# Merged weights written in place, two weight parts and a widening moved, in a GNN kernel

## What is computed

```
edge_index = stack([src, dst])
# layer 0
xw   = x @ W.T
deg  = segment_sum(1, col);  dinv = rsqrt(deg)
h    = segment_sum(dinv[row] * dinv[col] * xw[row], col) + b
x    = layernorm(x + gelu(batch_norm(h)) + x)
# layer 1, twice: basis1, att1 ... then basis2, att2 ...
w    = einsum('rb,bio->rio', att, basis)      # 2 relations from 30 matrices of 512 x 512
msg  = sigmoid(x[col] @ gate_w[r]) * x[col] @ w[r],  r by edge type
out  = segment_sum(msg, row) + x @ root + bias
```

## Time and profile before

| | before |
|---|---|
| median of three runs | 308.99 us (306.59 to 311.51) |
| the profiled execution, its own time | 306.44 us |
| its span, first to last instruction | 304.6 us |
| PE busy | 272.2 us (89%) |
| PE's weight loads busy | 180.6 us (59%) |
| DVE busy | 158.6 us (52%) |
| ACT busy | 87.9 us (29%) |
| POOL busy | 50.9 us (17%) |
| DMA, moved | 73.64 MB, mean 242 GB/s |
| mean granted clock of TensorE | 0.982 |

### The profile page before, as it was taken

The page is one execution under the profiler, slowest core; times in us unless marked ns, Lnnn a source line. Parts: engine busy times, 40 slices in busy tenths (PEclk is TensorE's granted clock), DMA queues, the critical chain, the costliest instruction groups (busy, mean ns, idle before and its releaser), DMA issues.

```text
span 304.6 us, 4601 instructions
## 1 busy us (share of the span) xinstructions
PE 272.2 (89%) x1687; PEld 180.6 (59%) x1687; DVE 158.6 (52%) x338; ACT 87.9 (29%) x143; POOL 50.9 (17%) x92
## 2 busy tenths in 40 slices
PE   0789997988999976679999999999998999999991
PEld 0673442443667632355766664677786777777770
DVE  6788889886647839835301413342342235334443
ACT  3351031002548694462440142114103252000000
POOL 5431013000590037100000000000008200011111
PEclk9999999999799998999999999999999999999997
DMA  6999999999499999959949797766003300001112
GB/s 155 219 413 373 381 421 413 396 396 386 174 310 332 421 420 421 352 224 347 377 183 390 281 418 292 290 267 270 2 0 87 88 1 0 0 2 34 34 34 67
DMA packets 12803, 73.64 MB, mean 242 GB/s; under 512 B 2000, under 2 KB 2243, under 8 KB 4588
## 3 DMA queue, kind: packets, MB, share of 16 engines
q1 hardware_dynamic: 11330, 70.82, 61.1%
q0 software_dynamic: 1104, 2.36, 3.0%
q10 hardware_dynamic: 346, 0.17, 0.3%
HBM read 72.05 MB, written 1.28 MB: 241 GB/s over the span
## 4 chain that ended last, share of the span: by engine, by line
PE 69%; DMA 11%; DVE 9%; issue 5%; DVEq 1%; ACT 1%; POOL 1%; SPq 0%; POOLq 0%; ACTq 0%
PE psW L552 15%; PE psM L533 9%; PE psM L534 9%; PE psM L535 9%; DMA basis_ring<-in_L_gnn_basis_dram 8%; PE psM L800 8%; PE psM L820 6%; PE psM L684 3%; DMA xs<-in_x_dram 3%; PE psM L607 2%; DVE B L1118 2%; PE psE L641 2%; PE psM L593 1%; PE psM L763 1%; DVE x_sum L1259 1%
## 5 line engine op out<-in xcount | busy, mean ns | idle before, releaser
L552 PE MATMUL psW<-basis_ring,S 128*32 128x512 f32 x512 | 65.1, 622 | 6.5 <-DMA basis_ring<-in_L_gnn_basis_dram 4.1
L1306 DVE SCALAR_TENSOR_TENSOR zg<-psM,gate,zg 125x512 fp32r<-125x512 f32 x20 | 15.0, 750 | 56.9 <-ACT zg L988 56.9
L552 PEld LDWEIGHTS psW<-basis_ring,S 128*32 128x32 f32 x512 | 13.2, 112 | 35.9 <-issue 21.9
L533 PE MATMUL psM<-w,hlT 128*125 128x512 f32 x80 | 32.4, 405 | 0.1
L534 PE MATMUL psM<-w,hlT 128*125 128x512 f32 x80 | 31.7, 396 | 0.0
L535 PE MATMUL psM<-w,hlT 128*125 128x512 f32 x80 | 31.7, 396 | 0.0
L988 ACT ACTIVATE zg<-psM,gate 125x512 fp32r<-125x512 f32 x20 | 13.8, 689 | 46.3 <-PE psM L535 45.9
L517 POOL DMA_DIRECT2D root_raw<-in_L_gnn_root_dram x16 | 7.9, 502 | 105.7 <-DVE hlT L1336 105.7
L641 PEld LDWEIGHTS psE<-oh_key,oh_src 128*125 128x125 f16 x162 | 14.0, 142 | 19.1 <-issue 12.7
L800 PEld LDWEIGHTS psM<-BB,zg 125*128 125x128 f32 x160 | 23.1, 188 | 3.4 <-issue 2.5
L800 PE MATMUL psM<-BB,zg 125*128 125x320 f32 (+1 forms) x160 | 24.1, 309 | 0.0
(11 more groups left out here) (154 smaller groups left out, 387.9 us busy)
## 6 DMA issues: line engine op xcount, KB each, us to landing
basis_ring<-in_L_gnn_basis_dram SPq DMA_DIRECT2D x64, 1024.0 KB, 7.3
root_raw<-in_L_gnn_root_dram POOLq DMA_DIRECT2D x32, 64.0 KB, 4.3
xs<-in_x_dram SPq DMA_DIRECT2D x1, 1120.0 KB
out_dram<-xs SPq DMA_DIRECT2D x5, 224.0 KB
w_raw<-in_L_gnn_W_dram SPq DMA_DIRECT2D x4, 256.0 KB, 9.7
bias_b<-in_L_gnn_bias_dram POOLq DMA_DIRECT2D x1, 250.0 KB, 3.8
xs<-in_x_dram SPq DMA_DIRECT2D x1, 130.0 KB
out_dram<-xs SPq DMA_DIRECT2D x5, 26.0 KB
```

Of the source, the lines that this page charges most:

```text
L533: nc.tensor.matmul(o, l_hi, r_hi, start=start, stop=False)
L552: m = nc.tensor.matmul(psW[32 * j:32 * j + 32, cc % 2, :], S[:, cc % 2, cc // CH, q].rearrange("p k r -> p (k r)"), ring[:, n % RING, j, : ...
L1306: link(v.scalar_tensor_tensor(out=zg[:, 1, c, r, :], in0=bank(("Z", L, c, r))[0:PC, :], scalar=gate[:, L, c, r:r + 1], in1=zg[:, 0, c, r, ...
```

## The change

- **In place.** `both` is gone. The merges write the full-width weights where the lower part will stand (`w03_full`, `w45_full` share memory with `w03`, `w45`), and already in the column order that blocks 0 to 3 need: the two merge instructions read `half` and `psW` with the step, and `w_high` and `w_low` read and write without one. The merge no longer waits for the upper and lower part of the block before; in its place DVE has the waits for the memory of blocks 4, 5 and from 6 on (`w_free`).
- **Lower part of block 0** goes from POOL (during the loop) to DVE, behind the sums of f = 0.
- **Parts on PE.** Parts 18 and 19 go from the loop (group 25) to behind the degrees, where 20 and 21 stood; 20 and 21 go behind f = 0, and 22 and 23 join 24 and 25 behind f = 1. Parts 10 and 11 move from group 15 to 14. Some steps of L607 and the transposes of the inputs are spread a little differently.
- **Counts widened first.** ACT widens chunks 1 to 3 ahead of copying the last chunk of x @ W.T out of PSUM, and DVE copies the degrees after the first instruction of merge 1, ahead of its other two.
- **Windows.** The registers of the four last windows are read in groups 1 and 13 in place of 0 and 1, and DVE waits for `base_i` one group later.
- **Way back.** The transposes of `hf` for chunks 0 to 3 go quarter by quarter: 16 transposes, of which the 13th is the first to complete a chunk. Chunk 4 follows.

In the diff, cut to its core:

```diff
-        both = sb("w_both", [P, 2, D], F32)
...
-        FIRST_IN = 23
+        FIRST_IN = 21
...
+        def w_full(pp, r):
+
+            b = pp % WBLK
+            return (w03_full[:, b] if b < 4 else w45_full[:, b - 4])[:, r, 1, :]
+
+        def w_free(eng, pp):
+
+            if pp == WBLK - 2:
+                eng.wait_ge(adj_used, T)
+            elif pp == WBLK - 1:
+                eng.wait_ge(root_ready, KC)
+            elif pp >= WBLK:
+                eng.wait_ge(main_full, uses[("Z", 0, NC - 1, R - 1)] + 1)
+
-        TURN_AT = {0: (AHEAD_OF_ATT + 1,), 1: (NC - 1,), 2: (NC, NC + 1), 3: (NC + 2, NC + 3)}
-        XW_AT = (0, 0, 0, 0, 0, 1, 1, 2, 2, 3, 5, 5, 6, 8, 9, 9, 10, 11, 11, 13, 13, 14, 14, 15, 17, 17, 17)
-        PARTS_AT = (0, 0, 0, 0, 2, 2, 4, 4, 6, 6, 6, 8, 8, 10, 10, 12, 12, 14, 14, 14, 16, 16, 18, 18, 18, 20, 20)
+        TURN_AT = {0: (AHEAD_OF_ATT,), 1: (AHEAD_OF_ATT + 1, NC - 1), 2: (NC, NC + 1), 3: (NC + 2, NC + 3)}
+        XW_AT = (0, 0, 0, 0, 0, 1, 1, 2, 2, 3, 5, 5, 6, 8, 9, 9, 11, 11, 12, 13, 13, 14, 14, 15, 17, 18, 18)
+        PARTS_AT = (0, 0, 0, 0, 2, 2, 4, 4, 6, 6, 6, 8, 8, 10, 12, 12, 12, 14, 14, 14, 16, 16, 18, 18, 18, 18, 18)
...
-            for r in range(R):
-                pool.wait_ge(w_hi, r + 1)
-                upper = w_block(0, 0)[:, r, 0, :].bitcast(F32)
-                nc.gpsimd.tensor_tensor(in_q(w_block(0, 0)[:, r, 1, :]), natural(both[:, r, :]), in_q(upper), ALU.subtract) \
-                    .then_inc(w_lo, 1)
...
-            basis_upto(21)
+            basis_upto(19)
...
-                basis_upto((None, FIRST_IN + 2, 27, 27)[f])
+                basis_upto((None, FIRST_IN + 4, 27, 27)[f])
             basis_upto(31)
-            for c in range(NC):
-                pe.wait_ge(gelu_done, KC)
-                wait_free(pe, ("g", c))
-                for f in range(KC):
...
+            for f in range(KC):
+                for c in range(NC - 1):
+                    way_back(f, c)
+            for f in range(KC):
+                way_back(f, NC - 1)
...
-            xw_out(4)
             for c in SUMMED:
                 act.wait_ge(at_sum, SUMMED.index(c) + 1)
                 nc.scalar.activation(AT[:, c], at_sums(c), ACT.Copy).then_inc(at_from_sum, 1)
+            xw_out(4)
...
-                dve.wait_ge(w_hi, R * pp)
-                dve.wait_ge(w_lo, R * pp)
-                v.scalar_tensor_tensor(out=both[:, 0, :], in0=psW[:, 1, :], scalar=mask_h[:, 1:2], in1=half[:, 0, :],
+                w_free(dve, pp)
+                to, first, second = w_full(pp, 0), half[:, 0, :], psW[:, 1, :]
+                if pp < KC:
+                    to, first, second = in_q(to), natural(first), natural(second)
+                v.scalar_tensor_tensor(out=to, in0=second, scalar=mask_h[:, 1:2], in1=first,
                                        op0=ALU.mult, op1=ALU.add).then_inc(w_both, 1)
...
-            w_merge(1)
+            w_merge_first(1)
             wait_full(dve, "deg")
...
+            w_merge_rest(1)
...
-                if f == 1:
-                    w_low(1)
+                if f < 2:
+                    w_low(f)
```

More of the change, by code:

```diff
@@ L717, in _, with way_back @@
                     counts_turned(2 * f + h)
-                basis_upto((None, FIRST_IN + 2, 27, 27)[f])
+                basis_upto((None, FIRST_IN + 4, 27, 27)[f])
             basis_upto(31)
-            for c in range(NC):
-                pe.wait_ge(gelu_done, KC)
-                wait_free(pe, ("g", c))
-                for f in range(KC):
-                    last[0] = nc.tensor.transpose(bank(("g", c))[0:PC, f * P:(f + 1) * P],
-                                                  hf[:, f, c * PC:(c + 1) * PC], ident[:])
-                done()
+            def way_back(f, c):
+                pe.wait_ge(gelu_done, f + 1)
+                if f == 0:
+                    wait_free(pe, ("g", c))
+                last[0] = nc.tensor.transpose(bank(("g", c))[0:PC, f * P:(f + 1) * P],
+                                              hf[:, f, c * PC:(c + 1) * PC], ident[:])
+                if f == KC - 1:
+                    done()
+            for f in range(KC):
[3 more added lines that the diff above has]
+                way_back(f, NC - 1)
             basis_upto(33)
@@ L1091, in w_merge_rest @@
                                             in1=half[:, 1, :], op0=ALU.mult, op1=ALU.add))
-                link(v.stream_shuffle(both[:, 1, :], half[:, 1, :], SWAPPED))
+                to, swapped = w_full(pp, 1), half[:, 1, :]
+                if pp < KC:
+                    to, swapped = in_q(to), natural(swapped)
+                link(v.stream_shuffle(to, swapped, SWAPPED))
                 dve.sem_inc(w_both, 1)
@@ L1099, in w_low @@
                     dve.wait_ge(w_hi, R * pp + r + 1)
-                    block_w = w_block(pp // KC, pp % KC)
-                    lo, full, hi = block_w[:, r, 1, :], both[:, r, :], block_w[:, r, 0, :].bitcast(F32)
-                    if pp < KC:
-                        lo, full, hi = in_q(lo), natural(full), in_q(hi)
-                    v.tensor_tensor(lo, full, hi, ALU.subtract).then_inc(w_lo, 1)
+                    upper, lower = (w_block(pp // KC, pp % KC)[:, r, i, :] for i in range(2))
+                    v.tensor_tensor(lower, w_full(pp, r), upper.bitcast(F32), ALU.subtract).then_inc(w_lo, 1)
             def window_at(w):
@@ L1134, in _ @@
                 one_hots(src.rearrange("p t (k i) -> p t k i", i=2), place_pairs, g * G, G, PLACES)
[L1136 to L1137 removed]
+                first, second = (2 * (g - 2), 2 * (g - 2) + 1) if g >= 2 else (NW - 4, NW - 3)
+                at = [window_at(first)] if g else []
                 one_hots(oh_key[:, g * G % OH:g * G % OH + G].rearrange("p t (k i) -> p t k i", i=2), key_pairs, g * G, G, KEYS) \
                     .then_inc(key_ready, 1)
[L1140 removed]
+                if g:
+                    at.append(window_at(second))
                 if g < 2:
```

29 lines of the change are left out of this document (10 added, 19 removed).

## The result

| | before | changed |
|---|---|---|
| median, first measurement, 4 runs each | 307.79 us (306.21 to 311.51) | 312.42 us (309.51 to 313.19) |
| ratio, 95% interval | | 1.0122 [1.0063, 1.018] |
| median, measured again (experiment e5), 23 and 12 runs | 310.08 us | 310.75 us |
| ratio, 95% interval | | 1.0033 [1.000, 1.0066] |
| profiled execution, own time / span | 306.44 / 304.6 us | 313.19 / 311.3 us; in e5 309.60 / 307.8 us |

A forecast was written before the change was run, and what follows sets the result against it. The stream of basis loads was taken as the bound up to 111 us. Load gap +1.7, root1 -0.9, way back +1.2, merges -0.7 and +0.6 gave +1.9 on the profiled 306.44: 308.3 us, range 303.5 to 312.5.

The forecast's parts named there:

- The gap: Pause in the basis loads near 77 us: grows from 3.8 to 5.5 or 6.5 us; +1.7 us taken, at full clock.
- rival 2: Low clock behind the degrees slows the aggregation, part 20 used after about 86 us, loads pause again: 311.3 us, chance 0.15.
- In the loop: Loop over the edges: DVE gains some 1.3 us, costed at nothing because part 17 lands at 64.37 regardless.
- From part 17 to part 18: PE up to the degrees' end: 25 matmuls take 2.86 us and end at 76.0 where it was 78.8.
- Root1: Its small loads between 83 and 98 us meet fewer basis parts: at best half of 3.6 us goes, -0.9 us taken.
- The way back: Transposes ahead of DVE's first `x_sum`: 13 needed instead of four, +1.2 us, which stay.
- Merges: Steps in DVE's merges: subtractions without the step win -0.7 us, merge instructions with it cost +0.6 us.
- Signs and range: Profile signs such as a load gap over 5 us and part 31 landing at 110.5 to 113; own range 306.8 to 310.5.
- Rival 1: PE's order, not the loads, ends last: PE stops waiting for parts 30 and 31, faster at 304.2 us, chance 0.25.

The follow-up runs named there:

- e5: The changed kernel run again unedited, on a second chip: 310.75 us, ratio 1.0033 to before.
- e2: The kernel before with only the places of parts 18 to 25 moved as in the change: 315.12 us, ratio 1.0129 to before.
- e11: The kernel before with merge 1's sums ahead of the degrees' copy and PE released ahead of the shuffle in every merge: 309.04 us, ratio 0.9959.
- e6: The changed kernel with root1's loads issued later, behind the scale of quarter f = 1: 317.61 us, ratio 1.0128 to before.
- e7: The changed kernel with parts 18 to 21 behind the degrees, 22 and 23 behind f = 0, 24 and 25 behind f = 1: 311.33 us, ratio 1.0083.
- e9: The changed kernel with parts at their places of before and the way back chunk by chunk, without earlier release of PE: 306.04 us, ratio 0.9872.
- e12: The kernel of e8 unedited, run again in another set: 303.92 us, ratio 0.9803 to before.
- e1: The changed kernel with only the parts put back at their places of before: 307.19 us, ratio 0.9899 to before.
- e10: The kernel of e8 with the change's new order of the way back: 304.80 us, ratio 0.9827 to before.
- e8: The changed kernel with parts and way back as before, and PE released ahead of the shuffle in every merge: 303.42 us, ratio 0.9773 to before.
- e3: The changed kernel with the way back chunk by chunk as before: 309.50 us, ratio 0.9992 to before.

## Why the prediction went wrong where it did

The direction was right, the size was not. Two steps of the prediction failed. The gap in the loads was priced with parts 18 and 19 at full clock, +1.7 us; they ran at half clock, and the pause grew by 2.9 us in one profile and by 4.4 us in the other. And four parts together behind f = 1 on a ring of four places were costed at nothing; PE waited 3.2 and 3.9 us for parts 24 and 25, and worked at half clock behind the wait.

The spans differ by 6.7 us in the first profile and by 3.2 us in e5's. Split at the landing of part 31 and at `x_sum`, in us against before:

| | forecast | changed | e5 |
|---|---|---|---|
| part 17 lands | 0 | -1.25 | -0.8 |
| first pause | +1.7 | +4.4 | +2.9 |
| second pause | (rival 2) | +1.8 | +1.3 |
| rest of the stream, root1 | -0.9 | -0.2 | -0.6 |
| part 31 lands | +0.8 | +4.75 | +2.8 |
| from there to `x_sum` | +1.2 | +1.0 | +1.0 |
| behind `x_sum` | -0.1 | +1.0 | -0.6 |
| sum | +1.9 | +6.7 | +3.2 |

The rows down to part 31 are an account of the stream of loads. The second pause is read off the DMA share from 106 to 110 us. "Rest" is what remains.

Read on PE, where the chain runs, the same +4.75 us is another sum. PE asks for part 24 at 94.57 us and not at 94.03, +0.5. It waits 3.9 us for parts 24 and 25. It no longer waits for parts 30 and 31 (0.8 and 1.4 us before), -2.3. What remains, +2.6 us, is work done at half clock behind the wait: part 25 takes 1.93 us and not 1.06, the next ten aggregation matmuls 3.04 and not 1.74. In e5 the four terms are -0.8, +3.2, -2.3 and +2.7, together +2.8.

**In the loop.** "Part 17 lands at 64.37 whatever DVE does" was wrong. It landed at 63.12 (63.58 in e5), PE did not wait for it in the first profile and only 0.40 us in e5. DVE's slow `oh_key` is gone, as forecast: the longest of the 27 takes 0.87 us, not 1.97. The loads come sooner step by step and not at one place: against before, part 5 lands 0.35 us sooner, part 9 0.73 and part 17 1.24. In all profiles with the changed kernel's loop part 17 lands between 62.2 and 63.6 us, in the three with the loop of before (before, e2, e11) between 64.0 and 64.6. Which edit of the loop does it was not tested.

**From part 17 to part 18.** Here the degrees' price failed in one profile of two. I took 2.86 us for the 25 matmuls and 76.0 as their end: they ended at 77.1 in the first profile and at 75.9 in e5. I had kept their duration of before, when the clock fell at 79 us, behind them. The clock fell earlier now, and in the first profile already within the degrees. The Trainium skill (TensorE: Matmul & The Clock Gate, Part 1) says that the place where the clock changes differs from run to run, and has measured it on the change to full clock. The prediction said that no run showed it; the two profiles of one kernel now show it of the fall, with 0.50 and 1.00 from 75 to 76 us. The same part of the Trainium skill has an idle array ahead of the fall; here PE was counted busy for 6.00 of the 6.00 us in which it fell, and in before's trace for 3.00 of 3.00 us at 0.50. So "the trace agrees on the drop" holds for the drop and not for an idle engine ahead of it.

**The gap.** Both prices for it were named, 5.5 us at full clock and 6.5 at half, and the full one taken, "as PE's thin stretch begins earlier but is shorter". That choice is the first failed step: parts 18 and 19 ran at half clock in both profiles (3.64 and 3.52 us for two, not 1.92). e5's 6.7 us is the half-clock price. The first profile's 8.2 us has the degrees at half clock on top.

**Root1.** The -0.9 us did not come in full. Its packets met parts 22 to 25 in place of 24 to 27, and 24 and 25 are the ones that PE now needs at once. They took 10.5 and 11.9 us to land; before, 26 and 27 had met them and took 9.2 and 11.8 us, and PE waited for neither. e6 shows the contention, and that its cost followed root1 to its new place.

**The second pause.** It looks like rival 2, with chance 0.15 and +3 us, but I had its trigger wrong, and it does not lie on the chain that ended last. It asked for part 20 used later than 86 us, behind a slow aggregation. Part 20 was used at 85.65, and at 84.33 in e5, and the pause came anyway. What I left out of the sum is the second failed step: four parts stand together behind f = 1, the ring has four places, so 24 can be issued only when 20 has been used (86.77), 7.8 us before PE asks for it (94.57), and the stream with root1 in it needs 10.5. Behind the wait there (3.9 us) the clock stands at 0.50, the next aggregation takes 3.04 us in place of 1.7, part 26 is used at 107.4, and part 30 is issued late. e7 shows that spreading the parts removes the second pause but not the loss.

**The way back.** Right in mechanism and nearly in size: +1.0 and not +1.2 us, as 13 transposes take 1.63 us. e9 and e12 against e1 and e10 show the same 1.0 us in the traces. e8, the kernel of e12 in another execution, has 1.39 us from part 31's last matmul to `x_sum` where e12 has 0.67, because there the gelu ends last. The sign that I gave, "about 2.2 us", did not fit my own sum (0.7 + 1.2 = 1.9); it measured 1.65. That "the 1.2 us stay" is right only where PE waits for part 31. In the changed kernel it doesn't, and e3 has the gelu end last, so the order there costs 0.16 us.

**Merges.** Right. It is the first merge instruction and the shuffle that read with the step; the second sum reads without it and still takes 0.75 us, so "the two merge instructions" under "In place" above is not exact. The first merge instruction takes 1.07 to 1.09 us where it took 0.75, the shuffle 1.01 to 1.05 where it took 0.73, and two subtractions 1.29 where they took 2.00. The Trainium skill (Vector Engine (DVE) Microarchitecture Reference, the SBUF access granule) has two sources that jump at each element as dear as one, for jumps of 4 KiB. The trace agrees for a step of 16 words, with one of the two sources in PSUM: 0.33 us more for 512 columns with two, 0.35 us with one. "PE's wait ahead of part 36 still over 2 us" was wrong for the first profile (0.87) and nearly right in e5 (1.81). The 0.87 is a wait shortened by a slower PE and not by DVE: in that execution the clock stood at 0.50 from 134 to 138 us, and parts 36 and 37 took 3.64 us for both. In e5 they took 1.92, at full clock. That is the nearest cause I have for +1.0 us against -0.6 behind `x_sum`, and it is not shown: e5 had a low stretch of its own there, with a clock of 0.53 and 0.62 from 124 to 128 us.

**Signs and range.** Of the signs that I had named, the gap of over 5 us came. Part 31 between 110.5 and 113 us did not (115.54 and 113.60), and PE not waiting for parts 30 and 31, a sign of being wrong, did come. The lower end of the forecast's own range, 306.8 us, needs the merges at no cost besides root1 at its best, which the text does not say.

**What I did not cost at all.** The merge that the change cuts in two releases PE only behind the degrees' copy. In the changed kernel this is hidden, since part 20 comes only at 85.65. In e1 it is a wait of 2.13 us. Nor did I see that the rest of the change is a gain of its own once the parts stand where they stood: e1 and e9 measured 0.990 and 0.987. Rival 1 had the direction, with the parts moved and for another reason. That the earlier degrees make this gain is likely but not shown, since no run has them alone.

**What stays open.** The size of the loss. 1.2% and 0.3% come from the same two kernels; each interval leaves the other's value out, and the intervals themselves just overlap, from 1.0063 to 1.0066. The earlier fall of the clock goes with a part 22 issued 1.5 us later in one profile than in the other, but I have not shown that it explains the two medians. The sets of experiments ran on different chips, and a difference between chips was not tested.

## What to carry to other kernels

When a consumer of a ring of n loads is moved behind other work, price the issue of part i + n and not only the use of part i, and count how many parts then stand together: as many as the ring has places means that the last of them were issued only one block of work ago. Give a moved stretch of thin matmuls both clock prices and follow the half-clock one into the next issue. And release a buffer at the last instruction that reads it: with the semaphore behind its third instruction the cut merge held PE up for 2.13 us in e1 and e9, and with it behind the second not at all in e8, e10 and e12. Last, read a loss on the chain that ended last and not only on the stream beside it: the second pause of the loads looked like 1.8 us and lay off the chain.

## What the runs showed of the hardware

- Two executions of one kernel on an unchanged instruction order had TensorE's clock fall about 1.3 us apart (granted 0.50 and 1.00 from 75 to 76 us), with PE counted busy throughout. In e6 it was at 0.50 from 74 to 76 us, and the degrees took 4.48 us. In the 14 profiles of this case the 25 matmuls took 2.86 to 2.89 us nine times and 3.33 to 4.48 us five times.
- Matmuls of 64 columns in place of 2 cost the same (2.89 and 2.86 us for 25), and the clock fell in that run too.
- With 16 loads of 64 KB beside the 1 MB loads the stream ran at 305 GB/s, for 16 us in e6, and at 422 GB/s behind them, at the same full share of the DMA engines. Before, it was 319 and 418.
- A shuffle of 512 columns that reads with a step of 16 words takes 1.01 to 1.05 us, and 0.73 without.
